# A graph kernel on Trainium2: the copy of x straight from DRAM to DRAM, and the sorts' order read and written at other places

## The chip, the cores and the metric

The kernel runs on one core of a Trainium2 chip. Times are device microseconds of one execution; the number to beat is the median of three executions. Five engines work side by side in a core: PE (matmul, with its weight loads as PEld), DVE (vector), ACT (scalar), POOL (GpSimd) and SP (sync); DMA transfers are issued from SP, ACT or POOL and run on the core's 16 DMA engines.

## The reference, cut to what matters

x has N = 50,000 rows of 256 f32; there are 12,500 edges (src, dst) with 128 features each; dst comes sorted, src does not.

```python
h = x @ Wn.T + bn;  e = edge_attr @ We.T + be
a = leaky_relu(((h[src] + e) * attn).sum(-1), 0.01)
a = softmax of a over the edges with the same dst
x = layernorm(x + relu(segment_sum(h[src] * a, dst)))
mean = segment_sum(x[dst], src) / max(count of src, 1)
out = layernorm(x + x @ W1.T + b1 + mean @ W2.T + b2)
```

So a row of z = x + relu(...) differs from x only where a node has an incoming edge (at most 12,500 of the 50,000 rows).

## The kernel before, in words

Edges are handled in T = 100 tiles of 128, in Q = 25 groups of four; nodes in G = 98 groups of 512 rows (128 partitions x 4 rows, 512 KB; the last has 84 partitions). The stages, in order:

- **z starts as a copy of x.** `z_scratch` lies in DRAM. `copy(n)` (L339 to L349) on SP moves n more groups: each is loaded into one of the four SBUF buffers `yout` (L344) and stored from it into z (L348), the store of group c - 2 behind the load of group c, with waits on the semaphores `s_cin` and `s_cout`. The pieces of the copy stand at several places of SP's program: four groups at the start, COPY_FIRST = 12 before the fifth chunk of edge features (L356), one after two of every three groups of the sorts' lookups (L381), COPY_ONEHOTS = 14 after the first group of the SRC sort (L380), the rest after the first two loads of sorted keys (L395).
- **Edge features.** SP loads 12 chunks of eight tiles (L360; each row piece is 512 B) and two single tiles (L366), the last of 84 rows; DVE forms a dot product for each tile (L790 to L803).
- **Two counting sorts**, first by dst (DST), then by src (SRC). DVE and ACT write one-hot tiles into X; PE counts them (`histogram`), and then goes through the 25 groups: for each group SP loads a row of low digits (L376, 128 KB, broadcast to 128 partitions) and of keys (L378, 256 KB), both double-buffered; PE adds each tile to a table and looks it up (L1179, L1228), DVE forms the ranks of the group (L846). POOL scatters each tile's records into `order_scratch` at their ranks (L473), FLIGHT = 4 at a time, one semaphore for each.
- **Order read back.** After the last DST scatter POOL loads `ordrow` (L484). In the SRC sort's lookups, at group ORDER_AT = 12, DVE turns it into index columns over three groups (L878 to L905).
- **Gathers.** POOL gathers the source rows of x into X, one indirect DMA for each tile, FLIGHT in flight (L492), each after PE has counted the SRC one-hots of that tile (`s_add`), which lie in the same place. DVE takes a dot product of each gathered tile (L1065).
- `order_src(20)` (L503) sends the first 20 of the SRC sort's 100 scatters. Then POOL waits for the whole copy of x (L504) and for `s_zero`.
- **Softmax**, then **by_dst**: 25 groups. SP loads the sorted keys (`load3`, L390), DVE makes selection matrices, PE aggregates and multiplies by Wn, ACT applies relu into `xin` (L680), POOL adds four tiles a group into z with an accumulating scatter (L513), each group after the scatters of the group before have landed, followed by two SRC order scatters.
- **The node pass** (`dense`): 98 groups; SP loads z (L407) and stores `out` (L412), DVE and ACT do both layernorms, PE the product with W1 + I. POOL sends what is left of the SRC order scatters, two for each group (L519), and loads `ordrow` again. At groups HOOK = 24, 26 and 28 DVE forms the SRC indices; from group HOOK + 8 on POOL gathers neighbour rows of z (L527), the 100 spread evenly over the groups up to G - 6, two in flight.
- **by_src**: 25 groups that gather own rows, aggregate, and scatter into `out`.

What sets the order of the work around the change: SP's program is in order, so a load stands behind every copy piece that is issued before it and behind the waits of `copy`; POOL's program is in order too. PE, DVE and ACT are tied by semaphores for each tile. The `[0:FT]` key rows (L332) have FT = 97 partitions.

Of the kernel before, what the change touches and what calls it, by code (L numbers as in the profile page):

```python
# [8 lines left out]
GT = 4  # L9
# [11 lines left out]
BF16 = mybir.dt.bfloat16  # L21
I32 = mybir.dt.int32
DST, SRC = 0, 1
ORDER_AT = 12
FLIGHT = 4
COPY_FIRST = 12
COPY_ONEHOTS = 14
HOOK = 24


def wait(eng, sem, value):

    if isinstance(value, int) and value <= 0:
        return
    eng.wait_ge(sem, value)
# [19 lines left out]
def build(nc, x, src, dst, edge_attr, Wn, bn, We, be, attn, W1, b1, W2, b2, out):  # L55
# [12 lines left out]
    assert 2 * HC <= 512 and LO == 2 * P and T % 4 == 0  # L68
    EC = 2 * GT
    NEC = FT // EC  # L70

    z_dram = nc.dram_tensor("z_scratch", [N + 6 * P, D], F32).ap()
    keyrow_dram = [nc.dram_tensor(f"keys_scratch{k}", [T, P], F32).ap() for k in (DST, SRC)]
# [4 lines left out]
    with ExitStack() as ctx:  # L78
# [6 lines left out]
        def sems(name, n):  # L85
            return [sem(f"{name}{i}") for i in range(n)]
# [142 lines left out]
        s_sortd = sem("sorted_keys_in_dram")  # L229
        s_xones = sem("ones_columns")  # L230
        s_xg = sems("src_rows_gathered", FLIGHT)
        s_cin = sems("copy_loaded", 4)
        s_cout = sems("copy_stored", 4)
        s_zero = sem("spare_rows_cleared")

        s_xin = sems("x_loaded", 4)
# [43 lines left out]
        s_enm = sem("edge_r_scales")  # L280
        s_ey = sem("edge_y_ready")
        s_xs = sems("own_z_rows_gathered", 4)
        s_nb = sems("neighbour_z_rows_gathered", 2)
        s_zsc = sems("z_rows_added", 4)
        s_ysc = sems("y_scattered", 4)
        s_rc = sems("reciprocals", 6)
# [29 lines left out]
        def parts(g):  # L316
            return LP if isinstance(g, int) and g == G - 1 else P
# [4 lines left out]
        def full(ap):  # L322
            return ap[:].rearrange("p j d -> p (j d)")
# [5 lines left out]
        def _(sp):  # L329
# [4 lines left out]
                sp.dma_start(xin[t][:, 0:2, :], w.rearrange("(b p) k -> p b k", b=2)).then_inc(s_w, 16)  # L334
            sp.dma_start(weT, We.rearrange("(b p) k -> p b k", b=2)).then_inc(s_w, 16)

            copied = [0]

            def copy(n):  # L339

                for c in range(copied[0], min(copied[0] + n, G + 2)):
                    if c < G:
                        wait(sp, s_cout[c % 4], 16 * (c // 4))
                        sp.dma_start(full(yout[c % 4])[0:parts(c)], grp(x, c, parts(c))).then_inc(s_cin[c % 4], 16)  # L344
                    if c >= 2:
                        h = c - 2
                        sp.wait_ge(s_cin[h % 4], 16 * (h // 4 + 1))
                        sp.dma_start(grp(z_dram, h, parts(h)), full(yout[h % 4])[0:parts(h)]).then_inc(s_cout[h % 4], 16)  # L348
                copied[0] = min(copied[0] + n, G + 2)  # L349

            copy(4)
            sp.wait_ge(s_wt, 3)
            sp.wait_ge(s_vu, 1)

            for c in range(NEC):
                if c == 4:  # L356
                    copy(COPY_FIRST)
                wait(sp, s_eau, EC * (c - 3))
                v = edge_attr[0:NEC * EC * P].rearrange("(c t p) d -> p c t d", p=P, t=EC)
                sp.dma_start(full(xin[c % 4]).rearrange("p (t d) -> p t d", d=DE),  # L360
                             v[:, c:c + 1].rearrange("p a t d -> p (a t) d")).then_inc(s_ea[c % 4], 16)
# [8 lines left out]
            for k in (DST, SRC):  # L370
                sp.wait_ge(s_keyd[k], 32)
                for q in range(Q):
                    n = k * Q + q
                    wait(sp, s_lbT, n - 1)
                    wait(sp, s_lbA, n - 1)
                    sp.dma_start(lowB[n % 2], spread(lowrow_dram[k], q)).then_inc(s_lb[n % 2], 16)  # L376
                    wait(sp, s_kbu, n - 1)
                    sp.dma_start(full(kB[n % 2]), spread(keyrow_dram[k], q)).then_inc(s_kb[n % 2], 16)  # L378
                    if k == SRC and q == 0:
                        copy(COPY_ONEHOTS)  # L380
                    elif q % 3:  # L381
                        copy(1)

            def load3(k, q):
                if k == DST and q < 2:
# [6 lines left out]
            sp.wait_ge(s_sortd, 16)  # L392
            for q in range(2):
                load3(DST, q)
            copy(G + 2)  # L395
            for q in range(2, Q):
                load3(DST, q)

# [25 lines left out]
        def _(pool):  # L424
# [38 lines left out]
            def gather(dst_ap, table, where, s):  # L463
                g.indirect_dma_start(out=dst_ap, out_offset=None, in_=table, in_offset=where).then_inc(s, 16)  # L464
# [36 lines left out]
                sent[0] = min(sent[0] + n, T)  # L501

            order_src(20)  # L503
            for u in range(4):  # L504
                pool.wait_ge(s_cout[u], 16 * len(range(u, G, 4)))
            pool.wait_ge(s_zero, 48)

            for q in range(Q):
                pool.wait_ge(s_relu, 2 * q + 2)
                if q:  # L510
                    pool.wait_ge(s_zsc[(q - 1) % 4], 16 * GT * ((q - 1) // 4 + 1))
                for j in range(GT):
                    g.indirect_dma_start(out=z_dram, out_offset=column(idx_out[DST], GT * q + j), in_=xin[q % 4][:, j, :],  # L513
                                         in_offset=None, compute_op=ALU.add).then_inc(s_zsc[q % 4], 16)
                order_src(2)

            for h in range((T - sent[0]) // 2):
                pool.wait_ge(s_x1, GT * h + GT)
# [4 lines left out]
            pool.wait_ge(s_agg[DST], T)  # L523
            for t in range(T):
                pool.wait_ge(s_x1, GT * (HOOK + 8 + (G - HOOK - 14) * t // T))
                wait(pool, s_nb[t % 2], 16 * (t // 2))
                gather(X[:, t, 0:D], z_dram, column(idx_dst[SRC], t), s_nb[t % 2])  # L527

            for q in range(Q + 3):
                if q < Q:  # L530
# [209 lines left out]
        def _(dve):  # L740
# [295 lines left out]
                ins.then_inc(s_nst, 1)  # L1036

            def first_neighbours():
                for par in range(2):
                    dve.wait_ge(s_nb[par], 16 * len(range(par, T, 2)))  # L1040
                for q in range(2):
                    neighbour_stats(q, q)

# [354 lines left out]
```

## Time and profile before

| | us |
|---|---|
| median of 3 executions | 1667.97 (1666.65 to 1668.83) |
| the profiled execution | 1660.1 |
| its span, first to last instruction | 1658.3 |
| busy: PE / PEld / DVE / ACT / POOL | 1265.2 / 1068.7 / 1094.4 / 782.0 / 750.0 |
| mean DMA rate over the span | 188 GB/s |

Busy times are of the profiled execution. A busy PE is not PE at its peak. The chain that ended last is by engine PE 44%, DMA 27%, POOL 12%, issue 8%, DVE 4%. In the stretches by stage the columns are: start:end, length, then for PE, PEld, DVE, ACT and POOL the busy time and in brackets the instructions, the granted TensorE clock as a share, the mean busy share of the 16 DMA engines, and GB/s. "To landing" is the time from the issue of a DMA to its last completion.

### The profile page before, as it was taken

What the parts mean: (1) busy time and instruction counts of PE and PEld (TensorE: products, weight loads), DVE (VectorE), ACT (ScalarE), POOL (GpSimd) and SP (SyncE); (2) the same over time, 40 slices, a digit from 0 to 9 for tenths busy, and PEclk for the clock granted to TensorE, in tenths of its full rate; (3) what the DMA queues carried; (4) which work ended last, traced back from release to release, by engine and by line L of the source; (5) the groups of instructions that cost most, each with busy time, mean ns of one, the idle gap of its engine ahead of it and who ended that gap; (6) DMA issues with size and microseconds to landing.
All of it is one profiled execution on the core that took longest, in us unless ns stands there. A gap on an engine that the chain in (4) does not pass through costs nothing.

```text
span 1658.3 us, 26818 instructions
## 1 busy us (share of the span) xinstructions
PE 1265.2 (76%) x7210; PEld 1068.7 (64%) x7210; DVE 1094.4 (66%) x3970; ACT 782.0 (47%) x1768; POOL 750.0 (45%) x731
## 2 busy tenths in 40 slices
PE   4277865776000799985099999999999899999994
PEld 3166754665000688764088888888888688877784
DVE  8565585666322655441088888888888888777762
ACT  6243475442000344332067777777777455444442
POOL 1035652035555678788642013333332256555553
PEclk9688798998555899999599999999999999999997
DMA  8977588767999555554557678888887323232221
GB/s 286 300 185 214 172 261 268 234 228 236 335 343 344 141 83 83 82 70 51 95 179 223 218 237 265 263 269 267 262 271 254 128 80 98 87 95 88 90 81 46
DMA packets 134006, 311.40 MB, mean 188 GB/s; under 512 B 24605, under 2 KB 57972, under 8 KB 133928
## 3 DMA queue, kind: packets, MB, share of 16 engines
q1 hardware_dynamic: 91870, 245.02, 44.7%
q0 software_dynamic: 40128, 64.45, 18.2%
q10 hardware_dynamic: 1930, 1.06, 0.2%
q8 instruction: 28, 0.46, 0.1%
q14 instruction: 50, 0.41, 0.1%
HBM read 182.23 MB, written 129.96 MB: 188 GB/s over the span
## 4 chain that ended last, share of the span: by engine, by line
PE 44%; DMA 27%; POOL 12%; issue 8%; DVE 4%; ACT 2%; SPq 2%; POOLq 0%; ACTq 0%
PE bank L1250 25%; DMA aggn<-low_digits_scratch 7%; DMA X<-in_x,idx_src 7%; PE bank L1240 6%; DMA z_scratch<-yout 5%; POOL z_scratch L513 4%; DMA xin<-z_scratch,idx_src 4%; POOL out_rows L467 4%; POOL xin L464 3%; PE bank L1247 3%; PE bank L1228 3%; DMA z_scratch<-xin,idx_out 3%; PE bank L1295 2%; PE bank L1291 2%; PE bank L1179 1%
## 5 line engine op out<-in xcount | busy, mean ns | idle before, releaser
L1250 PE MATMUL bank<-w1T,xT 128*128 128x256 f32 x1968 | 490.7, 380 | 0.0
L1250 PEld LDWEIGHTS bank<-w1T,xT 128*128 128x128 f32 x1968 | 343.3, 190 | 66.3
L473 POOL DMA_INDIRECT order_scratch<-pay,rank_i x200 | 196.8, 984 | 230.6 <-DVE rank_i L846 95.9
L568 ACT ACTIVATE yout<-bank,nmr,rstd 128x256 f32<-128x256 f32 x492 | 251.2, 576 | 8.0 <-DVE nmr L754 8.0
L919 DVE BATCH_NORM_STATS2 stats<-xin 128x6 f32<-128x512 f32 x246 | 158.7, 686 | 111.3 <-DMA xin<-z_scratch 57.6
L559 ACT COPY xT<-bank 128x512 f32<-128x512 f32 x346 | 203.0, 588 | 36.3 <-PE bank L1240 25.0
L464 POOL DMA_INDIRECT X<-z_scratch,idx_dst x100 | 94.9, 949 | 257.1 <-DVE xin L751 191.1
L919 DVE BATCH_NORM_STATS2 stats<-bank 128x6 f32<-128x512 f32 x246 | 168.5, 694 | 59.9 <-PE bank L1250 59.5
L667 ACT COPY agg<-bank 128x257 f32<-128x257 f32 (+1 forms) x200 | 74.2, 371 | 219.3 <-PE bank L1295 212.5
L513 POOL DMA_INDIRECT z_scratch<-xin,idx_out x100 | 158.2, 1582 | 40.7 <-issue 26.9
L1179 PE MATMUL bank<-X 128*128 128x196 bf16 x800 | 100.1, 261 | 99.0 <-ACT sel L654 72.8
L1228 PE MATMUL bank<-sel,agg 128*128 128x196 f32 x800 | 175.4, 369 | 0.0
L1240 PE MATMUL bank<-ident,xin 128*128 128x128 f32 x984 | 132.2, 274 | 53.1 <-DVE xin L751 53.1
L751 DVE TENSOR_SCALAR xin<-xin,stats,rstd 128x256 f32<-128x256 f32 x492 | 171.5, 410 | 1.0
L464 POOL DMA_INDIRECT X<-in_x,idx_src x100 | 97.1, 971 | 160.3 <-DVE idx_out L905 76.6
L563 ACT ACTIVATE std<-stats,eps_c 128x4 f32<-128x4 f32 x271 | 81.0, 300 | 182.0 <-DVE stats L919 173.8
L1247 PE MATMUL bank<-bias,ones 128*128 128x256 bf16 (+1 forms) x592 | 161.5, 273 | 3.0 <-ACT xT L559 2.7
L467 POOL DMA_INDIRECT out_rows<-yout,idx_out x100 | 99.9, 999 | 140.4 <-DMA xin<-z_scratch,idx_src 68.1
L1240 PEld LDWEIGHTS bank<-ident,xin 128*128 128x128 f32 x984 | 117.3, 142 | 68.3 <-issue 53.5
L1228 PEld LDWEIGHTS bank<-sel,agg 128*128 128x128 f32 x800 | 152.6, 218 | 0.3
L1179 PEld LDWEIGHTS bank<-X 128*128 128x128 bf16 x800 | 69.1, 102 | 128.2 <-ACT sel L654 86.5
L1295 PE MATMUL bank<-agg,csel 128*128 128x257 f32 (+1 forms) x396 | 123.4, 393 | 29.5 <-ACT agg L667 29.3
(187 smaller groups left out, 1911.7 us busy)
## 6 DMA issues: line engine op xcount, KB each, us to landing
yout<-in_x SPq DMA_DIRECT2D x97, 512.0 KB, 6.1
z_scratch<-yout SPq DMA_DIRECT2D x97, 512.0 KB, 7.1
xin<-z_scratch SPq DMA_DIRECT2D x97, 512.0 KB, 5.2
out_rows<-yout SPq DMA_DIRECT2D x97, 512.0 KB, 3.4
kB<-keys_scratch SPq DMA_DIRECT2D x50, 256.0 KB, 5.1
kB<-sorted_scratch SPq DMA_DIRECT2D x50, 256.0 KB, 3.4
aggn<-low_digits_scratch SPq DMA_DIRECT2D x50, 128.0 KB, 7.1
xin<-in_edge_attr SPq DMA_DIRECT2D x12, 512.0 KB, 7.1
```

The source lines that it names most:

```text
L464: g.indirect_dma_start(out=dst_ap, out_offset=None, in_=table, in_offset=where).then_inc(s, 16)
L473: g.indirect_dma_start(out=order_dram[k], out_offset=bass.IndirectOffsetOnAxis(ap=rank_i[k][:, t:t + 1], axis=0), in_=pay[:, t, :], in_off ...
L513: g.indirect_dma_start(out=z_dram, out_offset=column(idx_out[DST], GT * q + j), in_=xin[q % 4][:, j, :], in_offset=None, compute_op=ALU.ad ...
L559: a.copy(xT[dst_i][:].rearrange("p a b c -> p (a b c)"), src_bank[:, :]).then_inc(copied, 1)
L568: a.activation(yout[hu][0:rows, j, :], bank_of(j // 2)[0:rows, (j % 2) * D:(j % 2 + 1) * D], ACT.Identity, bias=nmr[0:rows, slot, j:j + 1] ...
L751: return v.tensor_scalar(o, i, s1, s2, o0, o1) if o1 is not None else v.tensor_scalar(o, i, s1, s2, o0)
L919: return v.bn_stats(stats[0:rows, slot, 2 * p:2 * p + 2, :].rearrange("p j s -> p (j s)"), pair.rearrange("p j c -> p c j"))
L1179: ins = mm(o[:, b * HC:(b + 1) * HC], onehot_lo[:, t, b * P:(b + 1) * P], onehot_hi[:, t, :], start=False, stop=False, skip_group_check=True)
L1228: ins = mm(bank[3 + t % 4][:, 0:HC], onehotT[n % 2][:, b, j * P:(j + 1) * P], table[i % 2][:, b, :], start=b == 0, stop=b == 1)
L1240: ins = tr(o[:, at:at + n], buf[0:n, 2 * p + jj, c * P:(c + 1) * P], ident[0:n, 0:n])
L1247: mm(to, ones16[:, 0:n], bias16[:, bias, :], start=True, stop=False)
L1250: ins = mm(to, buf[:, jj, c, 0:n], w[:, c, :], start=False, stop=i == len(terms) - 1 and c == 1)
```

## The change

The copy of x no longer passes through SBUF. It is cut into NCOPY = 100 transfers from DRAM to DRAM; transfer c takes rows 4c to 4c + 3 of every 400, so it has 125 pieces of 4 KB, one every 400 KB. No transfer waits for another; one semaphore, `s_copy`, counts all. Eight stand before the fifth chunk of edge features, 24 behind the loads of the second group of the SRC sort (two after each second group of one-hots), none among the lookups, and the last 68 behind the first two loads of sorted keys. DST's order is read at group 5 of the SRC lookups instead of 12, FLIGHT is 6 instead of 4, by_dst carries no order scatters, and so 80 of them are left for the node pass; HOOK moves from 24 to 48, and the neighbour gathers run from group 56 on instead of 32, four in flight instead of two.

```diff
@@ -21,11 +21,9 @@
 BF16 = mybir.dt.bfloat16
 I32 = mybir.dt.int32
 DST, SRC = 0, 1
-ORDER_AT = 12
-FLIGHT = 4
-COPY_FIRST = 12
-COPY_ONEHOTS = 14
-HOOK = 24
+ORDER_AT = 5
+FLIGHT = 6
+HOOK = 48
 
 
 def wait(eng, sem, value):
@@ -68,6 +66,8 @@
     assert 2 * HC <= 512 and LO == 2 * P and T % 4 == 0
     EC = 2 * GT
     NEC = FT // EC
+    NCOPY = 100
+    assert N % (NCOPY * GT) == 0
 
     z_dram = nc.dram_tensor("z_scratch", [N + 6 * P, D], F32).ap()
     keyrow_dram = [nc.dram_tensor(f"keys_scratch{k}", [T, P], F32).ap() for k in (DST, SRC)]
@@ -229,8 +229,7 @@
         s_sortd = sem("sorted_keys_in_dram")
         s_xones = sem("ones_columns")
         s_xg = sems("src_rows_gathered", FLIGHT)
-        s_cin = sems("copy_loaded", 4)
-        s_cout = sems("copy_stored", 4)
+        s_copy = sem("x_copied")
         s_zero = sem("spare_rows_cleared")
 
         s_xin = sems("x_loaded", 4)
@@ -280,7 +279,7 @@
         s_enm = sem("edge_r_scales")
         s_ey = sem("edge_y_ready")
         s_xs = sems("own_z_rows_gathered", 4)
-        s_nb = sems("neighbour_z_rows_gathered", 2)
+        s_nb = sems("neighbour_z_rows_gathered", 4)
         s_zsc = sems("z_rows_added", 4)
         s_ysc = sems("y_scattered", 4)
         s_rc = sems("reciprocals", 6)
@@ -334,27 +333,22 @@
                 sp.dma_start(xin[t][:, 0:2, :], w.rearrange("(b p) k -> p b k", b=2)).then_inc(s_w, 16)
             sp.dma_start(weT, We.rearrange("(b p) k -> p b k", b=2)).then_inc(s_w, 16)
 
-            copied = [0]
-
-            def copy(n):
-
-                for c in range(copied[0], min(copied[0] + n, G + 2)):
-                    if c < G:
-                        wait(sp, s_cout[c % 4], 16 * (c // 4))
-                        sp.dma_start(full(yout[c % 4])[0:parts(c)], grp(x, c, parts(c))).then_inc(s_cin[c % 4], 16)
-                    if c >= 2:
-                        h = c - 2
-                        sp.wait_ge(s_cin[h % 4], 16 * (h // 4 + 1))
-                        sp.dma_start(grp(z_dram, h, parts(h)), full(yout[h % 4])[0:parts(h)]).then_inc(s_cout[h % 4], 16)
-                copied[0] = min(copied[0] + n, G + 2)
-
-            copy(4)
             sp.wait_ge(s_wt, 3)
             sp.wait_ge(s_vu, 1)
 
+            copied = [0]
+
+            def part_of(table):
+                return table.rearrange("(r c k) d -> c r (k d)", c=NCOPY, k=GT)
+
+            def copy_x(n):
+                for c in range(copied[0], min(copied[0] + n, NCOPY)):
+                    sp.dma_start(part_of(z_dram[0:N])[c], part_of(x)[c]).then_inc(s_copy, 16)
+                copied[0] = min(copied[0] + n, NCOPY)
+
             for c in range(NEC):
                 if c == 4:
-                    copy(COPY_FIRST)
+                    copy_x(8)
                 wait(sp, s_eau, EC * (c - 3))
                 v = edge_attr[0:NEC * EC * P].rearrange("(c t p) d -> p c t d", p=P, t=EC)
                 sp.dma_start(full(xin[c % 4]).rearrange("p (t d) -> p t d", d=DE),
@@ -376,10 +370,10 @@
                     sp.dma_start(lowB[n % 2], spread(lowrow_dram[k], q)).then_inc(s_lb[n % 2], 16)
                     wait(sp, s_kbu, n - 1)
                     sp.dma_start(full(kB[n % 2]), spread(keyrow_dram[k], q)).then_inc(s_kb[n % 2], 16)
-                    if k == SRC and q == 0:
-                        copy(COPY_ONEHOTS)
-                    elif q % 3:
-                        copy(1)
+                    if k == SRC and q == 1:
+                        for i in range(Q // 2):
+                            sp.wait_ge(s_onehot, Q + 2 * i + 1)
+                            copy_x(2)
 
             def load3(k, q):
                 if k == DST and q < 2:
@@ -392,7 +386,7 @@
             sp.wait_ge(s_sortd, 16)
             for q in range(2):
                 load3(DST, q)
-            copy(G + 2)
+            copy_x(NCOPY)
             for q in range(2, Q):
                 load3(DST, q)
 
@@ -501,8 +495,7 @@
                 sent[0] = min(sent[0] + n, T)
 
             order_src(20)
-            for u in range(4):
-                pool.wait_ge(s_cout[u], 16 * len(range(u, G, 4)))
+            pool.wait_ge(s_copy, 16 * NCOPY)
             pool.wait_ge(s_zero, 48)
 
             for q in range(Q):
@@ -512,7 +505,6 @@
                 for j in range(GT):
                     g.indirect_dma_start(out=z_dram, out_offset=column(idx_out[DST], GT * q + j), in_=xin[q % 4][:, j, :],
                                          in_offset=None, compute_op=ALU.add).then_inc(s_zsc[q % 4], 16)
-                order_src(2)
 
             for h in range((T - sent[0]) // 2):
                 pool.wait_ge(s_x1, GT * h + GT)
@@ -523,8 +515,8 @@
             pool.wait_ge(s_agg[DST], T)
             for t in range(T):
                 pool.wait_ge(s_x1, GT * (HOOK + 8 + (G - HOOK - 14) * t // T))
-                wait(pool, s_nb[t % 2], 16 * (t // 2))
-                gather(X[:, t, 0:D], z_dram, column(idx_dst[SRC], t), s_nb[t % 2])
+                wait(pool, s_nb[t % 4], 16 * (t // 4))
+                gather(X[:, t, 0:D], z_dram, column(idx_dst[SRC], t), s_nb[t % 4])
 
             for q in range(Q + 3):
                 if q < Q:
@@ -1036,8 +1028,8 @@
                 ins.then_inc(s_nst, 1)
 
             def first_neighbours():
-                for par in range(2):
-                    dve.wait_ge(s_nb[par], 16 * len(range(par, T, 2)))
+                for i in range(4):
+                    dve.wait_ge(s_nb[i], 16 * len(range(i, T, 4)))
                 for q in range(2):
                     neighbour_stats(q, q)
```

## Rows read from the trace of the kernel before

**Rows 1.** Stretches by stage (columns as told above).
```profile
220.00:275.00 55.00, 33.61 (x269) 26.54 (x267) 38.51 (x194) 39.69 (x108) 27.50 (x28) 0.93 0.91 276
...
405.00:540.00 135.00, 4.66 (x29) 3.42 (x26) 45.90 (x232) 0.48 (x1) 71.38 (x74) 0.53 0.96 329
...
822.00:1300.00 478.00, 470.04 (x2752) 395.61 (x2752) 419.63 (x1098) 341.58 (x781) 139.50 (x148) 0.99 0.74 246
```

**Rows 2.** The chain that ended last: start us, us, what.
```profile
407.85 9.27 DMA X<-in_x,idx_src
...
527.77 6.50 DMA X<-in_x,idx_src
```

**Rows 3.** Line 513, all executions; below it POOL's timeline of one group.
```profile
L513 POOL DMA_INDIRECT z_scratch<-xin,idx_out x100: 1554/1572/1713, 564.0 to 818.3; - x100
...
DMA to landing us min/median/max: 3.7/3.9/5.4
...
699.60 1.61 POOL L513 DMA_INDIRECT z_scratch<-xin,idx_out  x1 [0.43 <-ACT xin L680]
...
705.25 1.55 POOL L513 DMA_INDIRECT z_scratch<-xin,idx_out  x1 [0.30 <-issue]
...
709.90 1.61 POOL L513 DMA_INDIRECT z_scratch<-xin,idx_out  x1 [0.51 <-ACT xin L680]
```

**Rows 4.** The page's DMA queues: SP's own queue.
```profile
q1 hardware_dynamic: 91870, 245.02, 44.7%
```

**Rows 5.** Timeline of the first 12 us: two key loads, DVE's first use.
```profile
1.13 0.35 SPq L332 DMA_DIRECT2D keyrow_i<-in_dst  x1
...
1.54 0.53 SPq L332 DMA_DIRECT2D keyrow_i<-in_src  x1
...
5.71 0.33 DVE L765 CAST keyrow_f<-keyrow_i 100x128 f32<-100x128 int32 x1 [0.42 <-DMA keyrow_i<-in_dst]
...
8.25 0.23 DVE L765 CAST keyrow_f<-keyrow_i 100x128 f32<-100x128 int32 x1 [1.70 <-DMA keyrow_i<-in_src]
```

**Rows 6.** DMA in 90 to 220 us: GB/s in 40 slices.
```profile
GB/s 38 113 387 69 57 354 180 342 88 38 344 273 283 79 45 239 352 272 116 2 124 400 328 152 13 45 343 393 189 45 49 260 379 235 96 31 157 363 285 179
```

**Rows 7.** Timeline of DVE in the first lookups: ranks of three groups.
```profile
171.40 0.15 DVE L846 TENSOR_TENSOR rank_i<-earlier,found 128x4 int32<-128x4 f32 x1
...
174.86 0.16 DVE L846 TENSOR_TENSOR rank_i<-earlier,found 128x4 int32<-128x4 f32 x1
...
181.73 0.15 DVE L846 TENSOR_TENSOR rank_i<-earlier,found 128x4 int32<-128x4 f32 x1
```

**Rows 8.** Line 846, both sorts; below it the first sort's last rank.
```profile
L846 DVE TENSOR_TENSOR rank_i<-earlier,found x50: 148/156/208, 96.3 to 408.8; 128x4 int32<-128x4 f32 x50
...
228.03 0.16 DVE L846 TENSOR_TENSOR rank_i<-earlier,found 128x4 int32<-128x4 f32 x1
```

**Rows 9.** Timeline of DVE: the SRC one-hots and the late low digits.
```profile
228.12 29.11 DVE L751 TENSOR_SCALAR X<-iota,dig_f 128x256 bf16<-128x256 bf16 x150
...
275.96 0.49 DVE L751 TENSOR_SCALAR agg<-aggn,slot_f 128x512 f32<-128x512 bf16 x1 [9.91 <-DMA aggn<-low_digits_scratch]
```

**Rows 10.** Line 360 (first to last issue); DVE at the fifth edge chunk.
```profile
L360 SPq DMA_DIRECT2D xin<-in_edge_attr x12: 367/646/3668, 18.3 to 76.6; - x12
...
69.52 0.29 DVE L754 SCALAR_TENSOR_TENSOR xin<-xin,u_b 128x128 f32<-128x128 f32 x1 [18.68 <-DMA xin<-in_edge_attr]
```

**Rows 11.** DVE's reading of the DST order; POOL's first gathers of x.
```profile
332.58 0.24 DVE L880 COPY krow<-ordrow 100x128 f32<-100x128 f32 x1
...
347.95 1.01 POOL L464 DMA_INDIRECT X<-in_x,idx_src  x1 [76.61 <-DVE idx_out L905]
...
351.81 0.95 POOL L464 DMA_INDIRECT X<-in_x,idx_src  x1 [0.30 <-issue]
353.07 0.95 POOL L464 DMA_INDIRECT X<-in_x,idx_src  x1 [0.31 <-PE bank L1179]
```

**Rows 12.** A stretch of the node pass beside the neighbour gathers.
```profile
1100.00:1258.00 158.00, 158.00 (x929) 133.24 (x928) 140.49 (x364) 116.06 (x266) 52.39 (x56) 1.00 0.80 266
```

## The prediction, made before the changed kernel had run

> **What bounds the kernel now.** I read the stages first, then the chain that ended last, then POOL's timeline and the DMA queue. The x rows go to z through four SBUF buffers: 98 groups, each loaded and stored by SP, all waited for before the first accumulating scatter into z. Beside the second sort's one-hots and beside the gathers of x the DMA engines are 0.91 and 0.96 busy, while PE is busy 4.7 of the latter 135 us [rows 1]. In those 135 us the chain is DMA landings of gathered rows: one every 7 to 9 us for four in flight, the last issued at 527.77 [rows 2]. 36 us later POOL adds into z: from 564.0 to 818.3 it issues 100 accumulating scatters of 1.55 to 1.61 us with 0.3 between, four per group, then two order scatters, 10.30 us per group (699.60 to 709.90) [rows 3]. Behind them the node pass is PE's: 470 of 478 us [rows 1]. So the end is set by when z can be scattered into; whatever moves 564.0 moves all behind it.
>
> **How many DMA engines a transfer gets.** This decides the case, and the page holds it. SP's queue q1 moved 91,870 packets [rows 4]. Its data packets follow from the code, one per contiguous piece of a row: x in, z out, z in, out 4 x (97 x 128 + 84) = 50,000; keys and sorted keys 100 x 128 = 12,800; low digits 50 x 128 = 6,400; edges 12 x 128 x 8 + 128 + 84 = 12,500; weights 1,024; key rows 2 x 97 = 194: 82,918. The other 8,952 are completion packets, one for each engine that took part. 562 transfers times 16 would be 8,992. Missing are 40 = 2 x 15 + 5 x 2: the two key loads of 97 rows ran on one engine, the five of 84 rows on 14. The split is the largest divisor of the row count up to 16. The clock agrees: the two key loads, issued 0.41 us apart, let DVE go at 5.71 and 8.25 [rows 5]: 49,664 B in 2.54 us, 19.6 GB/s, one after the other on the same engine.
> The new copy is 100 transfers with 50,000 / 400 = **125 rows** of 4 KB. 125 has the divisor 5: five engines, the same five each time. The Trainium skill, DMA: Bandwidth & Descriptors, section "Why a DMA increments its semaphore by 16 and not by 1", states this rule for every access pattern, DRAM sides included; no run yet shows it for DRAM to DRAM, and it speaks against this change.
>
> **Price of one copy, c.** With 16 engines the core moves up to 400 GB/s [rows 6], 25 per engine, 0.164 us per 4 KB. 25 packets on each of five engines: c = 25 x 0.164 = 4.1 us. That is the lower end (reading and writing overlap, as between DRAM and SBUF). The upper end is both legs one after the other, as the two transfers that it replaces: 8.2. I take 4.1: five engines ask little of a DRAM that serves sixteen.
>
> **Part by part.**
> 1. The early copies. Before, SP walks through 12 groups before the fifth edge chunk, and DVE waits for that until 69.52 [rows 10]. Now copy(4) is gone and 8 copies stand ahead of it: issued by 25 (the first edge chunk goes at 18.3), 8 x 4.1 = 33 on the five engines, and 5 for four edge chunks (1.3 each at 400 GB/s): DVE resumes at about 63.5. 6 us won.
> 2. First lookups. 25 groups, first rank at 96.3, last at 228.03 [rows 8]: 24 steps of 5.49. A step without a late load takes 3.46 (171.40 to 174.86), one behind a copy 6.87 (to 181.73) [rows 7]. Without copies 24 x (5.49 - 3.46) = 49 won: last rank at 228 - 6 - 49 = 173.
> 3. The one-hots' copies. 24 copies are issued at the pace of the one-hots (29 us [rows 9]), but take 24 x 4.1 = 98: done at 173 + 1 + 98 = 272. The loads for group 2 are issued behind them in the same queue and land at about 275. Before, the late load landed at 275.96 [rows 9]. The 55 won are given back.
> 4. Second lookups. Groups 2 to 24: 23 x 3.46 = 80, last rank at 355, before 408.8 [rows 8]: 54 won. SP's condition holds 3 us sooner, at 352.
> 5. Order at group 5. Before, it is read at 332.58 and the first gather comes 15.4 later [rows 11]. Now 275 + 3 x 3.46 = 286, and the first gather, as many but shorter steps later, at about 298; DST's scatters (100 x 1.26 from about 90, to 216) hide. At POOL's 1.26 a gather (351.81 to 353.07), with six in flight, the last is issued at 425: 103 earlier. Softmax and first products could let z start at 461.
> 6. **The last 68 copies**, from 352: two key loads 1.3, 68 x 4.1 = 279, and the five engines' part of 57 gathers: 8 KB each, 0.33, 19 us. With 2 us for landing and waking: **z starts at 653**, 89 later. The key loads for group 2 on stand behind them too; groups 0 and 1 have theirs and occupy POOL for 20 us.
> 7. POOL without order scatters: the next group still waits for the last landing, 3.9 after 705.25 [rows 3], so 709.15 in place of 709.90 at best. Between 0 and 0.75 for 25 groups; a load less in the queue is worth little, I take 0.2: 5 won.
> 8. The node pass takes 80 order scatters (two per 4.8 us group, done by group 40, read at 48) and 2.8 neighbour gathers a group for 1.7. POOL: 2.8 x 1.26 = 3.5 of 4.8. DMA share 0.80 [rows 12] rises to about 0.88; the three groups' lead of the loads hides it, without which some 5 us would come back. The last gather hangs on group 91 as before. Nothing.
> Sum: +89 - 5 = +84 on a span of 1658.3: 1742. The profiled execution took 1660.1, 1.8 more; the median is 1668.0, 7.9 above that. 1742 + 10 = **1752**.
> In general z starts at 276 + 92c; against 569 the copy breaks even at c = 3.2 us, that is, on seven engines or more.
>
> **Rivals.**
> A. *All sixteen engines after all* (the split is not by rows where both sides are DRAM, or moves on to other engines each time). For it: no such transfer is in the trace. Against: the two key loads took the same engine. c = 4.1 x 5/16 = 1.3: the copies vanish under the one-hots; first lookups end at 160, second at 160 + 37 + 86 = 283, the last gather is issued at 350, z starts at 388, copies done by 283 + 88 + 19 = 390. 390 - 564 - 5 = -179: 1489; with both legs c = 2.6, z at 283 + 177 + 19 + 3 = 482: 1581. This is the rival on the other side; it decides from c under 3.2.
> B. *Five engines, and both legs cost.* c = 8.2: early copies delay the edges to 96, 33 more; z at 276 + 754 + 33 = 1063: +494, **2162**. For it: each engine would have to read DRAM and write DRAM through one path. Against: loads and stores side by side reach 400 GB/s too.
> The Trainium skill, same page, section "Latency and other measured facts", gives 214 GB/s per direction for copies between two HBM tensors, with 128 rows; by five sixteenths of that (an estimate by the page) c would be 7.7 and the time about 2110. It stands on B's side if the limit is the engine's, on mine if it is the memory's; no row tells.
> C. *The gathers stay the bound* (the copies off the path, the gathers at the old (527.77 - 407.85) / 64 = 1.9 us each): 298 + 190 + 36 = 524, under 653, so it can decide only together with A.
>
> **Chances.** Forecast (c from 3.8 to 5) 0.52; between (5 to 7) 0.08; B 0.25; A 0.15. The likeliest case alone reaches from 1720 (c 3.9, 10 us from part 7) to 1835 (c 5). The range of 8 in 10 takes in B: 1715 to 2170; it leaves out A. Faster by over 0.2% (what a measurement of this kernel can tell): 0.14; same 0.02; slower 0.84.
>
> **What would show it.** Right: q1 with 5 completion packets a copy; DMA share near 0.3 and 120 to 130 GB/s when copies run alone; a landing at 272 to 280 for which DVE waited some 45 us in group 2; lookups then at 3.5 us; gathers issued every 1.26 us, the last near 425; PE idle until 650; the first scatter into z near 653 and the last 249 to 254 after it. Wrong: 0.9 shares during the copies (A); half the GB/s (B); lookups at 5 us without copies (then they had another bound, and part 2 falls); a node pass longer than 485.

## The result, and the profile after

The changed kernel takes **1771.53 us** (median of 4 runs, 1768.66 to 1773.04) against 1667.64 for the kernel before beside it (4 runs, 1666.65 to 1668.83): a ratio of 1.062, with a 95% interval of 1.060 to 1.064. Slower by 6%, in the range and near the forecast of 1752. In the profiled execution the span is 1769.6 us, 111.3 more than before. Where kernels are compared below, runs more than 1.5% above the fastest of the same kernel are set aside in the ratios.

The top of the changed kernel's page: the share of DMA engines and the rate by slice, the totals, the queue of SP, and the chain that ended last by engine and by line.

```profile
span 1769.6 us, 26717 instructions
...
DMA  4554333665333334555445666768888623332221
GB/s 141 171 100 106 113 125 112 185 193 201 132 132 132 132 140 82 82 87 76 55 53 183 222 219 217 227 218 282 293 296 300 226 66 95 91 91 88 90 84 47
DMA packets 118873, 260.18 MB, mean 147 GB/s; under 512 B 21973, under 2 KB 55340, under 8 KB 118796
...
q1 hardware_dynamic: 76738, 193.81, 32.8%
...
PE 45%; SPq 19%; DMA 10%; POOL 9%; issue 6%; DVE 6%; ACT 4%; ACTq 0%; POOLq 0%; DVEq 0%
```

SPq is SP's sequencer: a fifth of the chain is now the issuing of copies. **Five engines.** SP's queue moved 76,738 packets. Data: the 82,918 of before, less 25,000 (x in and z out by way of SBUF), plus 12,500 of 4 KB: 70,418. The other 6,320 are completion packets. 562 - 196 = 366 of the transfers of before are still there; 40 were missing to sixteen each [rows 4], 4 of them with the copy's load and store of 84 rows, which are gone: 366 x 16 - 36 = 5,820. That leaves 500 for 100 copies: five each. The Trainium skill, DMA: Bandwidth & Descriptors, section "Why a DMA increments its semaphore by 16 and not by 1", has that rule, and it holds here for DRAM to DRAM.

The stages of the changed kernel: start:end, length, busy time (instructions) of PE, PEld, DVE, ACT, POOL, then granted clock, DMA share, GB/s.

```profile
87.00:172.00 85.00, 78.01 (x529) 69.96 (x527) 72.04 (x397) 50.64 (x88) 62.32 (x64) 1.00 0.50 102
480.00:690.00 210.00, 17.78 (x85) 14.74 (x86) 11.85 (x47) 6.94 (x15) 11.78 (x8) 0.54 0.34 128
484.00:640.00 156.00, 0.00 (x0) 0.00 (x0) 0.00 (x0) 0.00 (x0) 0.00 (x0) 0.50 0.32 132
1200.00:1368.00 168.00, 168.00 (x987) 141.62 (x985) 150.52 (x387) 123.75 (x283) 93.63 (x99) 1.00 0.89 295
```

The third row is the change at its plainest: 156 us in which no compute engine runs an instruction. 0.32 of the DMA engines is five of sixteen; they move 132 GB/s, 26.4 each, so a copy of 512,000 B takes c = 3.88 us. In all the kernel moves 260 MB where it moved 311, with fewer packets, and is slower all the same; the first experiments test whether the number of engines is what counts.

SP's queue in the changed kernel, as a timeline: start us, us, what, how many [idle before <- releaser]; first behind the one-hots, then at the sorted keys, where the last row is POOL's first scatter into z.

```profile
178.19 0.32 SPq L372 DMA_DIRECT2D kB<-keys_scratch  x1
181.57 87.28 SPq L346 DMA_DIRECT2D z_scratch<-in_x  x24
268.96 3.44 SPq L370 DMA_DIRECT2D aggn<-low_digits_scratch  x1
...
380.88 0.80 SPq L384 DMA_DIRECT2D kB<-sorted_scratch  x2
381.73 270.51 SPq L346 DMA_DIRECT2D z_scratch<-in_x  x68
652.29 40.81 SPq L384 DMA_DIRECT2D kB<-sorted_scratch  x6
...
669.65 1.63 POOL L506 DMA_INDIRECT z_scratch<-xin,idx_out  x1 [200.87 <-DMA z_scratch<-in_x]
```

SP itself is held in the issue of 24 copies for 87 us and of 68 for 271. The low digits of group 2 were issued at 268.96, and DVE, in its timeline, got them at 286.33:

```profile
286.33 0.48 DVE L743 TENSOR_SCALAR agg<-aggn,slot_f 128x512 f32<-128x512 bf16 x1 [61.80 <-DMA aggn<-low_digits_scratch]
```

These are 17.4 us for a transfer of 128 KB. By 3.88 us a copy that is, as an estimate, some 4.5 copies ahead of it. Two waits answer to the last 68 copies in the list of waits (us in total, times, longest), beside the wait above as ACT has it:

```profile
POOL z_scratch L506 <- DMA z_scratch<-in_x: 200.9, 1, 200.9
DVE sel L743 <- DMA kB<-sorted_scratch: 200.1, 1, 200.1
ACT aggn L598 <- DMA aggn<-low_digits_scratch: 88.7, 4, 63.2
```

Last, the groups of the changed kernel that mark the stages: ns shortest/median/longest, first and last start (ranks of both sorts, gathers of x, scatters into z).

```profile
L838 DVE TENSOR_TENSOR rank_i<-earlier,found x50: 148/156/163, 89.4 to 382.8; 128x4 int32<-128x4 f32 x50
...
L458 POOL DMA_INDIRECT X<-in_x,idx_src x100: 942/947/1179, 314.0 to 442.5; - x100
...
L506 POOL DMA_INDIRECT z_scratch<-xin,idx_out x100: 1560/1561/1702, 669.6 to 928.1; - x100
```

The loss, against the stages of before [rows 3, 8]: z starts 105.6 us later (564.0 to 669.6); its scatters last 258.5 us, not 254.3: 4.2; from the last of them to the end 841.5, not 840.0: 1.5. Sum 111.3, the whole difference of the spans.

The 4.2 lie in the first steps. The second group of scatters, before and after:

```profile
574.13 1.69 POOL L513 DMA_INDIRECT z_scratch<-xin,idx_out  x1 [0.33 <-issue]
...
683.67 1.58 POOL L506 DMA_INDIRECT z_scratch<-xin,idx_out  x1 [6.75 <-ACT xin L672]
```

It comes 10.2 us behind the first group before, and 14.0 after, because POOL waits 6.75 us for ACT's relu. From the fourth group to the 25th a group takes 10.32 us before and 10.35 after.

### The profile page after: what moved, and what is told of

Its sections match the earlier page's. It is cut to its first block, busy times and chain, and to the rows that moved or that the text cites. A ratio compares the mean times of both kernels' runs of the same rounds, so it can differ in the third digit from the quotient of the medians.

```text
span 1769.6 us, 26717 instructions
## 1 busy us (share of the span) xinstructions
PE 1248.8 (71%) x7210; PEld 1051.0 (59%) x7210; DVE 1084.5 (61%) x3970; ACT 783.3 (44%) x1768; POOL 748.7 (42%) x731
## 3 DMA queue, kind: packets, MB, share of 16 engines
q1 hardware_dynamic: 76738, 193.81, 32.8%
## 4 chain that ended last, share of the span: by engine, by line
PE 45%; SPq 19%; DMA 10%; POOL 9%; issue 6%; DVE 6%; ACT 4%; ACTq 0%; POOLq 0%; DVEq 0%
PE bank L1242 25%; SPq L346 18%; PE bank L1232 7%; PE bank L1220 4%; POOL z_scratch L506 4%; DVE X L743 3%; DMA xin<-z_scratch,idx_src 3%; DMA z_scratch<-xin,idx_out 3%; PE bank L1239 3%; POOL out_rows L461 3%; PE bank L1287 3%; POOL xin L458 2%; PE bank L1283 2%; ACT aggn L598 2%; PE bank L1171 1%
## 5 line engine op out<-in xcount | busy, mean ns | idle before, releaser
L506 POOL DMA_INDIRECT z_scratch<-xin,idx_out x100 | 156.9, 1569 | 303.9 <-DMA z_scratch<-in_x 200.9
L1283 PE MATMUL bank<-X,sel 128*128 (+2 forms) x400 | 124.5, 395 | 198.6 <-DVE csel L743 198.6
L911 DVE BATCH_NORM_STATS2 stats<-xin 128x6 f32<-128x512 f32 x246 | 158.7, 687 | 111.3 <-DMA xin<-z_scratch 56.7
L1283 PEld LDWEIGHTS bank<-X,sel 128*128 128x128 f32 x400 | 69.2, 198 | 204.5 <-DVE csel L743 195.7
L1171 PE MATMUL bank<-X 128*128 128x196 bf16 x800 | 95.5, 253 | 102.6 <-ACT sel L646 77.7
L743 DVE TENSOR_SCALAR sel<-kB,keyc,weight 128x128 f32<-128x128 f32 x100 | 35.9, 360 | 200.7 <-DMA kB<-sorted_scratch 200.1
L1220 PE MATMUL bank<-sel,agg 128*128 128x196 f32 x800 | 157.0, 341 | 0.1
```

Source lines behind the costliest of these rows:

```text
L743: return v.tensor_scalar(o, i, s1, s2, o0, o1) if o1 is not None else v.tensor_scalar(o, i, s1, s2, o0)
L911: return v.bn_stats(stats[0:rows, slot, 2 * p:2 * p + 2, :].rearrange("p j s -> p (j s)"), pair.rearrange("p j c -> p c j"))
L1220: ins = mm(bank[3 + t % 4][:, 0:HC], onehotT[n % 2][:, b, j * P:(j + 1) * P], table[i % 2][:, b, :], start=b == 0, stop=b == 1)
L1283: ins = mm(o, sel[u % 2][:, j, :], rows, start=True, stop=first)
```

## The experiments

**First group: which part costs, and does it hang on the engines?** Beside these four the kernel before took 1660.1 us (median of 13).

*Ten engines.* Again 100 copies of 512,000 B, each of 100 pieces of 5 KB in place of 125 of 4 KB:

```diff
-    NCOPY = 100
-    assert N % (NCOPY * GT) == 0
+    NCOPY, KC = 100, 5
+    assert N % (NCOPY * KC) == 0
...
-                return table.rearrange("(r c k) d -> c r (k d)", c=NCOPY, k=GT)
+                return table.rearrange("(r c k) d -> c r (k d)", c=NCOPY, k=KC)
```

> The changed kernel with one number different: a transfer of the copy takes 5 rows of every 500 instead of 4 of every 400, so it has 100 pieces of 5 KB (512,000 bytes as before, 100 transfers as before), and 100 has the divisor 10. Theory S (the row count sets the number of engines, and an engine copies from DRAM to DRAM at 26 GB/s as in the changed kernel's 131 GB/s on five): 10 completion packets a copy, 262 GB/s and a DMA share near 0.65 where copies run alone, 1.95 us a copy. Copies behind the one-hots take 47 us, second lookups end near 330, the last 68 copies 133 us and the gathers' 19 beside them: first scatter into z near 481 instead of 670, time 1770 - 189 = about 1583, faster than before. Rival M (the memory or a path shared by all engines limits copies from DRAM to DRAM, and five engines are near it): GB/s stays near 131 to 150, time 1740 to 1770. Rival Q (the time comes from how the transfers queue, not from engines): no change, 1770.

Measured: **1580.49 us** (1577.08 to 1583.89), ratio 0.952 (0.943 to 0.961). Its queue, a window in which copies run beside the first groups of by_dst, and its scatters into z:

```profile
q1 hardware_dynamic: 74738, 193.81, 36.3%
...
392.00:460.00 68.00, 16.05 (x67) 11.65 (x67) 13.78 (x54) 5.57 (x13) 14.78 (x16) 0.60 0.64 260
...
L506 POOL DMA_INDIRECT z_scratch<-xin,idx_out x100: 1560/1561/1689, 479.8 to 738.5; - x100
```

10,000 data packets now, so 6,820 others: 1,000 beside the 5,820, ten for each copy. The rate doubles with the engines, the share too (0.64), and z starts at 479.8, where 481 was expected. A change of one number, 4 rows to a piece or 5, turns 6% of loss into 5% of gain.

*Sixteen engines.* 125 copies of 80 pieces of 5 KB, at the same places in the same proportion:

```diff
-    NCOPY = 100
+    NCOPY, KC = 125, 5
...
-                    copy_x(8)
+                    copy_x(10)
...
-                            copy_x(2)
+                            copy_x(2 + i % 2)
```

> The changed kernel with the copy cut into 125 transfers of 80 pieces of 5 KB (5 rows of every 625, 409,600 bytes each); 80 has the divisor 16. The places are kept, with as many bytes at each: 10 transfers, then 30, then 85. Theory S: 16 completion packets a copy; at 26 GB/s an engine 420 GB/s one way, 0.97 us a transfer; the copies vanish under the one-hots, lookups of the second sort start near 217 and end near 317, the last 85 transfers take 83 and the gathers' part 19: z near 421, and the gathers allow 414: time 1520 to 1530. Rival M (memory limits): the page of the Trainium skill on DMA has 214 GB/s per direction; then a transfer takes 1.9 us, the copies behind the one-hots 57, the last 85 163 us: z near 510 to 520, time 1610 to 1620. Rival Q: 1770.

Measured: **1540.80 us** (1537.53 to 1543.14), ratio 0.928 (0.922 to 0.935). Its queue; two windows, copies beside the first groups of by_dst, and copies beside the gathers; then the ranks and the scatters into z.

```profile
q1 hardware_dynamic: 75738, 193.82, 39.2%
...
388.00:424.00 36.00, 15.47 (x67) 11.12 (x67) 12.46 (x48) 5.57 (x13) 12.67 (x14) 0.69 1.03 313
320.00:375.00 55.00, 0.00 (x0) 0.00 (x0) 30.00 (x160) 0.00 (x0) 40.48 (x40) 0.51 1.02 376
...
L838 DVE TENSOR_TENSOR rank_i<-earlier,found x50: 148/156/161, 79.1 to 315.6; 128x4 int32<-128x4 f32 x50
...
L506 POOL DMA_INDIRECT z_scratch<-xin,idx_out x100: 1560/1561/1682, 442.4 to 699.7; - x100
```

Again 10,000 data packets, and 7,820 others: 2,000 beside the 5,820, sixteen for each copy. All engines are busy, but each moves 19.6 GB/s, not 26.4. The 5 KB pieces are not the cause, since ten engines moved them at 26 each; so at 313 GB/s something that the sixteen share seems to give out. What it is was not tested. The last 85 copies, 34.8 MB, and half the gathers, 6.4 MB, take 128 us from 314 to 442, where 16 x 26.4 GB/s would have made 98. So z starts later than expected, and the time is 11 us above the expectation's upper end. It is the quickest time measured here: 7% faster than before, 13% faster than the changed kernel. On two other chips that gain was not there (below).

*The copy alone*, everything else as before (groups of order scatters, HOOK, FLIGHT, two neighbour gathers):

```diff
-ORDER_AT = 5
-FLIGHT = 6
-HOOK = 48
+ORDER_AT = 12
+FLIGHT = 4
+HOOK = 24
...
+                order_src(2)
```

> The changed kernel with its copy as it is (five engines) and all the rest as before: order read at group 12, four in flight, HOOK 24, two order scatters a group in by_dst, neighbour gathers two in flight. Theory S: the copy alone makes the loss: the last gather comes near 500 to 540 and would let z start at 535 to 575, the copy lets it start at about 670, time 1765 to 1775. Rival R (the moved order scatters, HOOK or FLIGHT make a part of the loss): 1700 to 1755.

Measured: 1776.34 us (1773.86 to 1778.82), ratio 1.070 (1.061 to 1.080).

```profile
L506 POOL DMA_INDIRECT z_scratch<-xin,idx_out x100: 1554/1572/1709, 676.0 to 934.9; - x100
```

*The rest alone*, with the copy by way of SBUF back at its old places and the order, FLIGHT, HOOK and node pass as changed:

> The kernel before with its copy through SBUF and all the rest as changed: order read at group 5, six in flight, HOOK 48, no order scatters in by_dst. Theory S: gathers start near 312 and are done near 450, then the copy through SBUF is what z waits for: 37 groups from 409 at 3.5 us a group, done near 545 instead of 553: z at about 550 instead of 564, the stage of scatters 250 to 254, time 1640 to 1658. Rival R (the rest costs time by itself, in the node pass or by late refilling of by_dst): 1670 to 1690.

Measured: 1645.05 us (1636.93 to 1648.96, 10 runs), ratio 0.993 (0.990 to 0.995).

```profile
L513 POOL DMA_INDIRECT z_scratch<-xin,idx_out x100: 1560/1560/1684, 539.1 to 796.3; - x100
```

What POOL waited for ahead of its first scatter into z:

```profile
POOL z_scratch L513 <- DMA z_scratch<-yout: 73.5, 1, 73.5
```

The two halves: the copy makes the whole loss (and a little more), the rest gains 12 us by the ratio. Its gathers are issued by 439.3, not 527.8, so z no longer waits for them; it waits 73.5 us for the copy by way of SBUF, and that sets 539.1 instead of 564.0.

**Second and third group: what is each part worth once the copy is quick?** These eight ran on chips where the kernel before itself took longer, 1741.8 us (19 runs) beside the first four and 1727.2 (7 runs) beside the others; times and starts are compared within a group only, and the expectations that are written for the first chip can be judged only by differences.

*Sixteen engines, the rest as before* (the two diffs above together):

> The copy on sixteen engines (as in the run with sixteen) and all the rest as before: order at group 12, four in flight, HOOK 24, order scatters in by_dst, neighbour gathers two in flight. Theory S: once the copy is quick the gathers are the bound and the earlier order counts: first gather near 282 instead of 246.8, four in flight beside busy engines 1.9 us each from 315 on, last gather near 456, z near 492 instead of 442: time about 1590. Rival (the rest is worth as little here as alone, where it gave 0.7%): 1541 to 1555.

*Sixteen engines, with two order scatters a group in by_dst* (`order_src(2)` back, HOOK left at 48):

> Sixteen engines, with the two order scatters of each by_dst group put back (HOOK stays at 48). Theory S: the next group waits for the landing of the last accumulating scatter, 3.8 us after its issue, and the two scatters of 1.3 us lie in that wait: stage of scatters 257 to 259 us as without them (257.3), time within 4 us of 1541. Rival P (they cost POOL's 2.6 us a group, or a part of it): 20 to 65 us more.

Measured: with the rest as before 1773.27 us (1772.14 to 1774.39, two runs), ratio 1.023 (1.013 to 1.033); with order scatters in by_dst 1748.16 (1729.15 to 1760.76, 10 runs), ratio 1.004 (0.999 to 1.009). So on this chip neither is faster than the kernel before. The ranks and POOL's wait of the first, then the ranks, the scatters and the same wait of the second:

```profile
L839 DVE TENSOR_TENSOR rank_i<-earlier,found x50: 153/156/163, 78.6 to 476.9; 128x4 int32<-128x4 f32 x50
POOL z_scratch L506 <- DMA z_scratch<-in_x: 69.5, 1, 69.5
...
L839 DVE TENSOR_TENSOR rank_i<-earlier,found x50: 151/156/161, 78.2 to 444.0; 128x4 int32<-128x4 f32 x50
L506 POOL DMA_INDIRECT z_scratch<-xin,idx_out x100: 1555/1572/1682, 554.5 to 813.1; - x100
POOL z_scratch L506 <- DMA z_scratch<-in_x: 81.5, 1, 81.5
```

258.6 us from first to last scatter, against 257.3 without the order scatters (sixteen engines, first group). So order scatters in by_dst are nearly free and their removal gains nothing. The 25 us between the two kernels are not the gathers, as the expectation had it: in both, z waits for the copy, 69.5 and 81.5 us long. With the rest as before z starts 31 us later (585.5), because the last rank falls 33 us later. Shortly behind the reading of the order two of its lookup groups take 90.0 us together, where two take 52.3 in the other kernel; no releaser is named for these halts (below). The two differ in ORDER_AT, FLIGHT, HOOK and the neighbour gathers in flight; no run takes these apart.

*The 24 copies behind the one-hots sent at the end* instead, on five engines, as changed otherwise:

```diff
-                    if k == SRC and q == 1:
-                        for i in range(Q // 2):
-                            sp.wait_ge(s_onehot, Q + 2 * i + 1)
-                            copy_x(2)
```

> The changed kernel, five engines, without the 24 copies behind the SRC one-hots; they go with the last ones, 92 in place of 68. Theory S (the loads of the second sort's group 2 stood behind those 24 in SP's queue): DVE's wait of 61.8 us is gone, last rank near 317 instead of 382.8, last gather near 380; but the five engines lose the 104 us in which they worked, 92 x 3.9 = 358 and 16 for the gathers from 315: z near 690 to 695, time 1790 to 1797, slower than the changed kernel although the lookups end 65 us earlier. Rival F (that wait has another cause): last rank stays near 383, z near 760, time 1860.

Measured: 2000.21 us (1988.07 to 2012.36), ratio 1.154 (1.138 to 1.171). A window of copies alone, and the scatters into z:

```profile
700.00:790.00 90.00, 0.00 (x0) 0.00 (x0) 0.00 (x0) 0.00 (x0) 0.00 (x0) 0.50 0.32 132
...
L502 POOL DMA_INDIRECT z_scratch<-xin,idx_out x100: 1560/1561/1681, 820.7 to 1076.6; - x100
```

The five engines move 132 GB/s on this chip too. DVE's wait of 61.8 us in group 2 is gone, but the 92 copies now go from 454.19 to 820.7, 366 us, where 68 took 288 in the changed kernel, 16 of them for gathers that no longer run beside: 24 copies more for 95 us, 3.96 each. The wait removed in front was 61.8, so by this sum the late copies lose some 30 us, and what ran while DVE and ACT made one-hots was free. That is an estimate over two chips: the changed kernel itself was not run on this one. The time is 200 above the expectation, which was written for the first chip; 140 of these stand in the last rank, at 457.0 where 317 was expected.

*Sixteen engines, copies among the lookups too*, one after each group from the third on:

```diff
                             copy_x(2 + i % 2)
+                    elif q > 1:
+                        copy_x(1)
```

> Sixteen engines, and one transfer of 400 KB behind the loads of each group of lookups from the third on in both sorts (23 and 23), so 39 instead of 85 are left for the end. Theory S: a transfer of 1 us ahead of a load that has some 5 us of lead costs nothing, steps stay near 3.9 us, second lookups end at 315 to 325, copies are done near 365, and z waits for the gathers: last gather near 378, z near 415, time about 1515. Rival L (a copy beside the lookups delays the loads as it did before): steps of 4.5 us or more, z at 450 or later, time 1550 or more.

Measured: 1723.79 us (1704.68 to 1735.92, 10 runs), ratio 0.991 (0.986 to 0.995). Its ranks, its scatters into z, and what they waited for:

```profile
L840 DVE TENSOR_TENSOR rank_i<-earlier,found x50: 151/156/164, 77.6 to 442.3; 128x4 int32<-128x4 f32 x50
L508 POOL DMA_INDIRECT z_scratch<-xin,idx_out x100: 1560/1561/1681, 523.2 to 776.6; - x100
...
POOL z_scratch L508 <- ACT xin L674: 96.2, 15, 52.2
```

The copy has left the path: the first scatter waits 52.2 us for the relu of its own group, not for x. Beside the kernel with order scatters in by_dst, the nearest on this chip, the last rank falls at the same place (442.3 and 444.0), z starts 31 us earlier and the median is 24 us lower. Sixteen engines without spreading had not run on this chip, so both ran again on a third, with the order scatters and the late copies:

> The kernel with sixteen engines once more, beside the next three: the chip of the four runs before gave the kernel before 1742 us instead of 1660 to 1668, so they are to be compared on one chip. If the chip gives the kernel before 1660 to 1675: 1535 to 1545, z near 442.

> Sixteen engines with one 400 KB transfer behind the loads of each lookup group from the third on. On the slower chip z no longer waited for the copy but for the first relu. Theory S: z near 415 to 420 instead of 442, time 1513 to 1522, 20 to 28 us under the run with sixteen beside it; steps of the lookups within 0.2 us of 3.85. Rival L (copies beside the lookups delay the loads, as before): steps of 4.5 or more and no gain.

> Sixteen engines with the two order scatters of each by_dst group put back. Theory S: they lie in the wait for the landing, stage of scatters within 2 us of the run with sixteen beside it, time within 4 us of it. Rival P: 20 to 65 us more.

> The changed kernel (five engines) with the 24 copies of the one-hots sent at the end, on whatever chip this is. On the slower chip the wait of 61.8 us was gone and 92 transfers took 365 us from SP's release to the first scatter into z. Theory S on a chip like the first: last rank near 317, z near 690, time 1790 to 1797. Rival F: last rank near 383, time 1860.

| third group | all runs, us | median of those compared | z scatters |
|---|---|---|---|
| before | 1727.20 (1677.56 to 1749.18) | 1679.33 (3 of 7) | |
| sixteen engines | 1733.38 (1683.17 to 1749.26) | 1683.17 (1 of 4) | 561.4 to 820.4 |
| sixteen, spread | 1700.38 (1689.36 to 1708.08) | 1700.38 (4 of 4) | 530.5 to 783.5 |
| sixteen, order in by_dst | 1744.29 (1722.92 to 1750.44) | 1743.75 (3 of 4) | 556.0 to 814.7 |
| five, late copies | 1952.01 (1930.76 to 1973.27) | 1930.76 (1 of 2) | 811.4 to 1067.3 |

In the traces the spread copies again start z 31 us earlier, while the last rank falls at 447.1 with them and at 445.7 without:

```profile
L838 DVE TENSOR_TENSOR rank_i<-earlier,found x50: 149/160/167, 78.7 to 445.7; 128x4 int32<-128x4 f32 x50
```

```profile
L840 DVE TENSOR_TENSOR rank_i<-earlier,found x50: 152/160/169, 78.5 to 447.1; 128x4 int32<-128x4 f32 x50
```

So on these chips copies beside the lookups do not lengthen them, and they bring z forward. That this shortens the kernel is open: the second group's medians speak for it (24 us), but in the third the one run of sixteen engines that is compared took 1683.17, less than any run of the spread version. Order scatters in by_dst again cost nothing in their stage (258.7 us against 259.0). The late copies repeat: 366.6 us for 92.

But sixteen engines, 7% faster than before on the first chip, are no faster than before here (1733 and 1727, or 1683.17 and 1679.33), and on the second chip three kernels with the sixteen-engine copy had ratios of 1.023, 1.004 and 0.991. What differs shows in the trace with order scatters in by_dst of the second chip, beside the one of sixteen engines of the first. Its span is 206.6 us longer: 57 more in the ranks of the first sort, 76 in those of the second, 93 behind the last scatter into z, and 20 less between these stages. A group of the first sort takes 6.15 us there on the mean, not 3.77. In the second sort the groups up to the reading of the order take what they take on the first chip, then one takes 43, the next 9, and the rest 6.0 on the mean. The engines stand idle meanwhile without a releaser that the profile names, as the list of waits of the same trace has it, where the one of the first chip has no "remote" at all:

```profile
ACT sel L647 <- remote: 78.3, 19, 25.5
DVE bank L747 <- remote: 55.9, 19, 9.7
...
PE bank L1172 <- issue: 35.3, 16, 18.7
```

The kernel before may suffer less since its steps of 5.49 us [rows 8] held late loads already, under which a part of such idle time hides; that is argued, not shown, since there is no trace of it on these chips. What the idle time is stays open, and so does whether the spread version would beat 1540.8 us on a chip like the first: it was not run there.

## Why the prediction was right, step by step

The sign, the mechanism (five engines, by the divisor of 125) and the size hold: 1742 was forecast for the span, 1769.6 came. The missing 27.3 us are 16.6 in the start of z, 9.2 in its stage, 1.5 behind. The lower end of the likeliest case, 1720, does not follow from its own terms: c = 3.9 and 10 us from part 7 give 1729.

- **c = 4.1**: measured 3.88. Reading and writing overlap, so rival B (8.2) falls. So does the estimate of 7.7 that was worked out from the 214 GB/s of the Trainium skill, DMA: Bandwidth & Descriptors, section "Latency and other measured facts". Rival A falls by the five packets per copy. What it would have given was tried by other row counts: z at 442 and 1540.8 us with sixteen engines, between its two estimates of 1489 and 1581. The break-even of 3.2 was not tried itself; ten engines (1.97 us for 512,000 B at 260 GB/s) lie well below it and win.
- **Part 1**: DVE resumed at 61.69 (forecast 63.5).
- **Part 2 is the step that was mis-sized.** The last rank of the first sort fell at 180.2, not 173: a lookup step without late loads takes 3.78 us on the mean, not 3.46. The one step that I took as typical (171.40 to 174.86) [rows 7] came right behind a late one and caught up; a mean over steps would have been needed. PE and DVE are busy 78 and 72 of 85 us in that stage: under the loads lay another bound, close by.
- **Part 3**: the 55 us were given back, as forecast, and 11 more: group 2's first one-hot at 286.33, not 275. The copies started 7.6 later, and from there to the landing it was 105 us, not 101.
- **Part 4**: last rank at 382.8, not 355: 11.3 from part 3, and 16.5 from the steps. From the landing to the last rank it took 96.5 us, 24 steps of 3.95 and 1.8 to the first, where 23 of 3.46 were forecast.
- **Part 5**: gathers from 314.0 to 442.5, 1.30 us each (forecast 298 to 425, 1.26): late by parts 3 and 4, but off the path: POOL then waited 200.9 us for the copy. So rival C did not come into play.
- **Part 6**: SP was released at 381.7, 29.7 later than forecast, but needed 288 us from there, not 301 (c was smaller). z at 669.6, not 653. "Occupy POOL for 20 us" was too kind: the first four groups went at 669.65, 683.67, 693.85 and 705.17, 14.0, 10.2 and 11.3 us apart, where a step took 10.3 before: the sorted keys of group 2 on came only after the copies, and PE, which had waited for them, brought the second group's products late.
- **Part 7 failed.** A gain of 5 us was forecast for the order scatters' removal; there was none (10.32 us a group before, 10.35 after), and the stage got 4.2 longer by its first steps, as told under part 6. The scatter of the next group waits for the landing of the last, about 3.8 us after its issue, and the two order scatters lay inside that wait, which was the forecast's own lower bound of 0. Two experiments put them back: 258.6 and 258.7 us, against 257.3 and 259.0 without.
- **Part 8**: nothing was forecast; the node pass and by_src took 1.5 us more. The DMA share beside the neighbour gathers (1200.7 to 1368.6) is 0.89, against 0.80 before [rows 12]; 0.88 was forecast. It cost nothing that the total shows.

## What to carry to other kernels

Count the rows of a transfer before anything else: with 125 it runs on five DMA engines, with 100 on ten, with 80 on sixteen. The kernel with five engines in its copy was 6% slower than the one with the detour through SBUF, and in the first group it was 5% faster with ten and 7% faster with sixteen; the rest of the change alone is worth 0.7%. The completion packets of the queue (here 5, 10, 16 a copy) show the number in one subtraction. On two other chips the gain of sixteen was gone, so measure such a gain on more than one chip. And a transfer that nobody waits for still holds up what is issued behind it in the same queue: five slow engines made the lookups, the sorted keys and z wait in turn.

## What was not expected of the hardware

- One DMA engine copies DRAM to DRAM at 26.4 GB/s, about what it moves between DRAM and SBUF [rows 6]; the leg back costs nothing more. Five and ten engines scale (132 and 260 GB/s); sixteen reach 313, 19.6 each, and 376 in all beside gathers into SBUF. The Trainium skill, DMA: Bandwidth & Descriptors, section "Latency and other measured facts", gives 214 GB/s per direction as the full rate of a copy of 128 rows of 16 KiB between tensors in DRAM. The rate of 313 measured here, for 80 rows of 5 KB, is higher and decides.
- The queue held an estimated 4.5 copies of 500 KB ahead of a load (17.4 us at 3.88 us a copy on five engines), while SP itself was held 87 us in issuing 24 copies.
- The kernel before took 1660, 1742 and 1727 us on three chips, and the one with sixteen engines 1541 and 1733 us on two. In the two traces compared above the lookups are 133 us longer and what lies behind the scatters into z 93, in part as idle time without a named releaser.
